# Reciprocal root of a gated recurrence output: quarter-size tile spread by DMA, multiply on GpSimd instead of a combined gate

## What is computed

```python
gg = (x @ Wg.T).reshape(B, L, H, DH)
o = o * jax.lax.rsqrt(jnp.mean(o * o, -1, keepdims=True) + EPS)
o = o * o_norm_w * jax.nn.silu(gg)
return (o.reshape(B, L, KEY_DIM) @ Wo.T, final_state)
```

## Time and profile before

| | us |
|---|---|
| median of 3 runs | 1225.5 (1222.16 to 1226.76) |
| profiled execution | 1221.33 |
| its span | 1219.5 |
| PE busy | 1145.7 (94%) |
| DVE busy | 814.1 (67%) |
| ACT busy | 716.0 (59%) |
| POOL busy | 499.3 (41%) |

### The profile page before, as it was taken

One profiled execution on the slowest core, in us unless ns is written; L12 is line 12 of the kernel. 1 busy time (PEld: TensorE's weight loads), 2 busy tenths in 40 slices (PEclk: granted clock), 3 DMA queues, 4 the chain that ended last, 5 costly groups with the idle time before them and its releaser, 6 DMA issues.

```text
span 1219.5 us, 30002 instructions
## 1 busy us (share of the span) xinstructions
PE 1145.7 (94%) x12192; PEld 790.1 (65%) x12192; DVE 814.1 (67%) x1454; ACT 716.0 (59%) x1212; POOL 499.3 (41%) x709
## 2 busy tenths in 40 slices
PE   7888899999999999999998989859999999999987
PEld 2444455555555555555555556649998998998976
DVE  4897667768768768668576665665665566655552
ACT  3776467677677676776775866624444434445433
POOL 1659576575675774773774811100011000001000
PEclk9999799999999999999998999989999999999999
DMA  3123222323323223243326422161111122111100
GB/s 118 46 52 79 66 52 60 107 58 72 87 58 93 68 73 77 77 128 89 91 73 150 151 62 72 47 235 45 44 45 49 50 52 70 44 44 48 30 17 10
DMA packets 134602, 88.07 MB, mean 72 GB/s; under 512 B 79264, under 2 KB 118048, under 8 KB 133568
## 3 DMA queue, kind: packets, MB, share of 16 engines
q1 hardware_dynamic: 133312, 85.93, 25.9%
q10 hardware_dynamic: 1152, 0.21, 0.1%
HBM read 54.77 MB, written 14.55 MB: 57 GB/s over the span
## 4 chain that ended last, share of the span: by engine, by line
PE 75%; POOL 8%; DVE 5%; issue 4%; ACT 3%; SPq 2%; DMA 2%; ACTq 0%; POOLq 0%; DVEq 0%
PE proj L467 20%; PE out L1494 5%; PE turned_v_chain L1494 5%; PE gram L482 4%; PE turned_v_chain L1560 4%; PE proj L1552 4%; PE proj L1433 4%; POOL inverse L1204 3%; POOL rank_one L1201 3%; PE out L491 2%; PE turned_v_chain L596 2%; PE gram L1468 2%; PE decays L497 2%; PE turned_v_chain L629 2%; DVE conv L992 2%
## 5 line engine op out<-in xcount | busy, mean ns | idle before, releaser
L992 DVE SCALAR_TENSOR_TENSOR conv<-proj,kq_weights,conv 128x504 f32<-128x504 f32 (+2 forms) x261 | 189.9, 731 | 24.4 <-ACT conv L736 17.7
L467 PE MATMUL proj<-xT,vg_weights 128*128 128x512 f32 x384 | 190.6, 620 | 1.8 <-DVE conv L992 1.6
L1791 POOL TENSOR_TENSOR rope<-rope_part,rope_part 128x512 f32<-128x512 f32 x32 | 40.0, 1271 | 364.8 <-DVE rope_part L1730 364.8
L992 DVE SCALAR_TENSOR_TENSOR conv<-proj,vg_weights,conv 128x504 f32<-128x504 f32 (+2 forms) x192 | 140.8, 734 | 44.9 <-ACT conv L736 40.0
L467 PE MATMUL proj<-xT,kq_weights 128*128 128x512 f32 x348 | 164.5, 599 | 0.2 <-DVE conv L992 0.2
L1204 POOL TENSOR_TENSOR inverse<-inverse,rank_one 128x30 f32<-128x30 f32 (+14 forms) x240 | 125.2, 522 | 18.8
L1201 POOL TENSOR_TENSOR rank_one<-inverse 128x30 f32<-128x30 f32 (+14 forms) x240 | 117.7, 490 | 15.9
L467 PEld LDWEIGHTS proj<-xT,vg_weights 128*128 128x128 f32 x384 | 68.4, 192 | 65.6 <-issue 59.8
L467 PEld LDWEIGHTS proj<-xT,kq_weights 128*128 128x128 f32 x348 | 62.4, 190 | 72.8 <-issue 70.3
L1569 ACT ACTIVATE rstd<-rstd 128x1 f32<-128x1 f32 x48 | 9.8, 203 | 142.6 <-DVE rstd L1677 142.6
L482 PEld LDWEIGHTS gram<-keys_q 128*64 128x64 f32 x896 | 57.6, 138 | 54.7 <-ACT keys_q L747 36.4
(11 more groups left out here) (244 smaller groups left out, 2464.0 us busy)
## 6 DMA issues: line engine op xcount, KB each, us to landing
kq_weights<-in_kq_w SPq DMA_DIRECT2D x32, 390.0 KB, 3.5
vg_weights<-in_vg_w SPq DMA_DIRECT2D x32, 390.0 KB, 4.0
o_scratch<-oT SPq DMA_DIRECT2D x32, 256.0 KB, 2.9
o_in<-o_scratch SPq DMA_DIRECT2D x16, 512.0 KB, 4.1
diagonal<-gram_decayed SPq DMA_DIRECT2D x128, 32.0 KB, 1.9
inverse<-inverse SPq DMA_DIRECT2D x32, 128.0 KB, 2.7
q_first<-rope SPq DMA_DIRECT2D x128, 32.0 KB, 1.9
q_second<-rope SPq DMA_DIRECT2D x128, 32.0 KB, 1.9
```

The costliest lines, as they stand in the source:

```text
L467: mm = e.matmul(bank(c, u)[:], w[:, (k * 3 + c % 3) * 128:(k * 3 + c % 3 + 1) * 128], xT[g][:, k, :], start=(k == 0), stop=(k == KD - 1))
L992: e.scalar_tensor_tensor(acc(c, u)[:, :, back:], src[:, :, 0:S - back], weights(c, u)[:, j:j + 1], acc(c, u)[:, :, back:], ALU.mult, ALU.a ...
L1791: e.tensor_tensor(turned[half][:].rearrange("p b r q -> p r b q"), parts[2 * half][:], parts[2 * half + 1][:], op).then_inc(s_turned, 1)
```

## The change

The root no longer goes into the gate. DVE forms `oT` from `OB`, `o_norm_w` and the gate alone, and no longer waits for the root. The sum over partitions is made by four matmuls of 32 output partitions, each for 128 of the 512 columns, so that Ln and Exp run on a 128x128 tile (`rs4`) whose four blocks of 32 partitions hold the four quarters. Four DMAs of SP spread one row of each block over all 128 partitions of `o_rs`. POOL then multiplies `oT` by `o_rs` in all of slots 11 to 42, behind the first part of its elimination cut. The store of `oT` waits for that product, as do the tile phase's waits in PE and ACT (and a new one in DVE). SP's four DMAs stand first in its slot; one kind of preparation store (KRS) moves from the end of a slot to the next slot, behind them.

```diff
@@ sync @@
                 for s in range(SLOTS):
+                    if live(uo):
+                        e.wait_ge(s_rs, uo + 1)
+                        wait(e, s_gr, uo)
+                        for j in range(4):
+                            e.dma_start(o_rs[:, j * TILE:(j + 1) * TILE],
+                                        rs4[RB * j:RB * j + 1, None, :].broadcast_to([1, 128, TILE])).then_inc(d_rs, 16)
+                    rotated = prepare_at(s - 1)
+                    if rotated is not None and rotated[1] == KRS:
+                        prepare_store(*rotated)
                     if live(ua + 1):
...
                     if live(uo):
-                        e.wait_ge(s_og, uo + 1)
+                        e.wait_ge(s_gr, uo + 1)
                         e.dma_start(o_scratch[:, 4 * group(uo):4 * group(uo) + 4, head(uo), :],
...
-                    if now is not None:
+                    if now is not None and now[1] != KRS:
                         prepare_store(*now)
@@ tensor @@
                 def norm(u):
                     e.wait_ge(s_osum, u + 1)
-                    e.matmul(VB, ones_mean[:], o_sum[:], start=True, stop=True).then_inc(s_norm, 1)
+                    for j in range(4):
+                        mm = e.matmul(VB[rows(j), 0:TILE], ones_mean[:, 0:RB], o_sum[:, j * TILE:(j + 1) * TILE],
+                                      start=True, stop=True)
+                    mm.then_inc(s_norm, 1)
@@ scalar @@
                 def silu_gate(u):
-                    wait(e, s_gr, u - 2)
+                    wait(e, s_og, u - 2)
...
                         e.wait_ge(s_norm, uo + 1)
-                        wait(e, s_og, uo)
-                        e.activation(o_rs[:], VB, ACT.Ln, scale=float(2 ** O_SHIFT), bias=guard[:, 0:1]).then_inc(s_ln, 1)
+                        wait(e, d_rs, 64 * uo)
+                        e.activation(rs4[:], VB[:, 0:TILE], ACT.Ln, scale=float(2 ** O_SHIFT), bias=guard[:, 0:1]).then_inc(s_ln, 1)
...
-                        e.activation(o_rs[:], o_rs[:], ACT.Exp, scale=-0.5).then_inc(s_rs, 1)
+                        e.activation(rs4[:], rs4[:], ACT.Exp, scale=-0.5).then_inc(s_rs, 1)
@@ vector @@
-                def scale_gate(u):
-                    e.wait_ge(s_rs, u + 1)
-                    e.wait_ge(s_silu[G], u + 1)
-                    wait(e, s_og, u)
-                    e.tensor_tensor(o_rs[:], flat(gate[u % 3]), o_rs[:], ALU.mult).then_inc(s_gr, 1)
...
                     def gate_output():
-                        if s > U:
-                            scale_gate(uo)
-                        e.wait_ge(s_gr, uo + 1)
+                        e.wait_ge(s_osq, uo + 1)
+                        e.wait_ge(s_silu[G], uo + 1)
...
-                        e.scalar_tensor_tensor(oT[uo % 2][:], OB[:], onorm[:, 0:1], o_rs[:], ALU.mult,
+                        e.scalar_tensor_tensor(oT[uo % 2][:], OB[:], onorm[:, 0:1], flat(gate[uo % 3]), ALU.mult,
                                                ALU.mult).then_inc(s_og, 1)
@@ gpsimd @@
-                    if live(uo) and s <= U:
-                        e.wait_ge(s_rs, uo + 1)
-                        e.wait_ge(s_silu[G], uo + 1)
-                        wait(e, s_og, uo)
-                        e.tensor_tensor(o_rs[:], flat(gate[uo % 3]), o_rs[:], ALU.mult).then_inc(s_gr, 1)
...
                     elif solving:
                         eliminate(h, CUTS[cut][0])
                         if cut == 3:
                             scale_columns()
+                    if live(uo):
+                        e.wait_ge(s_og, uo + 1)
+                        e.wait_ge(d_rs, 64 * (uo + 1))
+                        e.tensor_tensor(oT[uo % 2][:], oT[uo % 2][:], o_rs[:], ALU.mult).then_inc(s_gr, 1)
@@ tile phase: tensor at u4 == 0, scalar at u3 == 0 @@
-                                e.wait_ge(done["o"], U)
+                                e.wait_ge(done["scaled"], U)
@@ tile phase: vector @@
+                        if u3 == 0:
+                            e.wait_ge(done["scaled"], U)
```

7 lines of the change are left out of this document (4 added, 3 removed).

## The result

| us | before | after |
|---|---|---|
| median | 1223.8 (4 runs, 1220.7 to 1226.8) | 1265.9 (4 runs, 1265.3 to 1267.2) |
| ratio after/before, 95% interval | | 1.035 (1.032 to 1.038) |
| profiled execution, its span | 1221.33, 1219.5 | 1267.19, 1265.4 |

Slower, with 1260 forecast and 1230 to 1285 as the range. The medians lie 42 us apart and the two profiled spans 45.9 us, because the profile before is of one of that kernel's fastest executions (its median was 1223.8 to 1226.8 in five groups of runs) and the profile after is of the slowest of four. First the busy line of the page after, for the earlier trace rows; then the table by stretch, for the earlier trace rows and for stretches behind it (columns: stretch, its length, busy time of PE, PEld, DVE, ACT, POOL, PE clock, DMA share, GB/s).

A forecast was written before the change was run, and what follows sets the result against it. PE was taken to bound slots 10 to 31, POOL's chain the stretch up to 705.4 us, and ACT, PE and DVE in turn past 789. -11.0 + 21.8 - 3.5 + 27.2 = +34.5 us: 1255.8 profiled, 1260 as median, range 1230 to 1285.

The forecast's parts named there:

- Slots 37 to 41: Five shorter norm pieces give 2.5 us, PE's shorter waits for DVE about 1: -3.5 us; late weights could give 3 back.
- rival 2: One port for all reads: transfers 2.5 us longer, counted twice in each late stretch, +10 us, 1270; chance 17%.
- Four column tiles: PE in slots 10 to 31: four side by side take 0.44 us, a gain of 0.5 per unit, -11 us for 22.
- Rival 5: Column tiles don't run side by side: +14 us on any outcome, 1274 on the forecast; no chance of its own given.
- It costs nothing, if the four DMAs have landed.: Slots 10 to 31: POOL's multiply fits the idle time before its o_sum addition; the DMAs may take about 13 us.
- The four DMAs, 9.5 us: 9.5 us from first issue to last landing on an empty queue, 7.0 more behind a full one.
- Rival 1: Short DMAs: the four take 4.5 us; still slower, +12 us, median 1237; chance 17%.
- Slots 33 to 36, POOL's chain, +21.8: Late DMAs, the second unit's queued behind large loads, delay POOL's multiplies and elimination: +21.8 us, as the chain is POOL's alone.
- Slots 41 and 42, +27.2: The last unit's DMAs land behind 5 MB of weights, so multiply, attT and nope(2) come late: +27.2 us.
- the sign of ACT idle for 28 us: Sign that the forecast is right: ACT idle some 28 us before L1624.
- Rival 3: Faster: small transfers slip past the large loads and the DMAs are waited for nowhere; median 1214; chance 9%.
- Rival 4: DMAs well over 13 us: norm waits in each of 22 slots, each further us costing 22; chance 4%.

The follow-up runs named there:

- experiment 7: Changed kernel with the four DMAs of slots 11 to 32 issued behind the key and value weights instead of ahead of them; 1267.8 us.
- experiment 9: Changed kernel with eight DMAs of 64 columns in place of four of 128 columns in slots 11 to 32; 1271.8 us.
- experiment 6: Changed kernel with each of the four DMAs reading all 128 partitions of the quarter tile instead of one partition 128 times; 1238.1 us.
- experiment 10: Changed kernel with unit 23 alone (scaled in slot 34) given one 128x512 sum, full-width Ln and Exp and no DMAs; 1259.8 us.
- experiment 12: Against the kernel with unit 23 alone repaired: thirteen large loads moved from the end of slot 33 to behind slot 34's value weights; 1255.4 us.
- experiment 2: Changed kernel with one 128x512 sum, full-width Ln and Exp and no DMAs from slot 33 on, POOL still multiplying; 1213.1 us.
- experiment 4: Changed kernel with SP's large loads moved behind the spread of slot 34 and behind the last spread of slot 42; 1257.6 us.
- experiment 8: Changed kernel with units 30 and 31 alone (slots 41 and 42) given one 128x512 sum, full-width Ln and Exp, no DMAs; 1239.7 us.
- experiment 5: Changed kernel with the four DMAs of slots 33 to 42 issued by ACT in its own queue instead of by SP; 1259.3 us.

## Why the prediction was right, and where its sizes were off

Direction, places and the mechanism of the three large terms were right: a small gain on PE, then two late stretches where a spread lands behind large loads. Slots 37 to 41 were forecast with the wrong sign. Of the 10 us by which the sum misses, some 4 are the choice of the two profiled executions. By number alone, 1265.9 lies nearer to rival 2's 1270 than to 1260. By its terms, on the profiled scale (the two traces also start 1.4 us apart):

| term | predicted | measured |
|---|---|---|
| slots 10 to 31 | -11.0 | -9.2 |
| slots 32 or 33 to 36 | +21.8 | +17.7 |
| slots 37 to 41 | -3.5 | +6.9 |
| slots 41, 42 to the end | +27.2 | +29.1 |
| sum | +34.5 | +44.5 |

- **Four column tiles.** 0.44 us predicted. The next piece starts 0.36 us behind `norm` and itself takes 0.10 longer (622.64 - 620.73 against 608.24 - 606.43), together 0.46. In pairs the eight products of 0.11 us alone would take 0.44, so more than two ran side by side. "TensorEngine Tiling (Array Packing)" of the Trainium skill, section "Theoretical Speedup", allows up to four times for 32 columns, and the trace agrees with that. Rival 5 falls. With a wide source the same slots gain 11.1 us against the kernel before (492.2 to 481.1), the predicted 11; the missing 1.9 us go to the next point.
- **"It costs nothing, if the four DMAs have landed."** Nearly so. The 13 us of cover were counted from an ordinary slot. In one slot of four SP starts the spread 4 to 6 us late, and there no cover is left. That is 1.9 us in all by one profile of each (0.9 to 3.7 by the eight), and the next microsecond of delay costs at once (experiments 7 and 9: 5 to 6 us).
- **The four DMAs, 9.5 us.** 10.3 us in a quiet slot. With 4.4 us for the shortest landing the others follow at (10.3 - 4.4)/3 = 1.97 us, 33 GB/s, where I had 37; in slot 38 the landings come 1.8 to 2.1 us apart. The Trainium skill's page "SBUF — State Buffer", section "Door 1: The DMA port swizzle", has 27.6 GB/s, from which I estimated 11.9 us for four; the trace lies between, and experiment 6 shows the read of one partition to be the cause. Rival 1 falls since the four took 10.3 us and not 4.5; rival 2's size was too large, its mechanism, a slow read side, is the right one.
- **Slots 33 to 36, POOL's chain, +21.8.** The chain was late as predicted (scaling at 659.36, 8 us of lead eaten; the wait of 10 us in slot 34), and it was the bound at slot 37: DVE waited 7.6 us for it. The size was 4 us too large, since the spread landed 11.6 us behind its issue at 672.8, where the prediction has 16.1 (679.7 to 695.8). (A slip without weight: the 8.0 us count from the store, at 657.9, and not from the 658.6 that the text names.) What the step missed is that the chain was not alone. PE's wait for value weights behind the same loads is nearly as late. Without POOL's wait slot 37 starts 10.6 us sooner (experiment 10); without PE's as well it starts no sooner (12), since POOL's chain, held from its start by unit 22's spread, is the bound again.
- **Slots 37 to 41, -3.5.** This step failed, by 10.4 us. It put late weights at 3 us, and those only in the range; they cost about 6. In slot 40 PE waits 3.0 us for value weights and its next group of matmuls takes 3.49 us and not 1.98 (first row below). These weights were issued at 769.11 and landed 8.2 us later; the same ones took 3.3 us in experiment 6, where the spread reads 128 partitions, and nothing waited for them. From the start of slot 37 to the `norm` of slot 42 the kernel of experiment 6 took 80.7 us and experiment 2, without late spreads, 80.9. The changed kernel took 86.9, and experiments 4, 7, 8, 9 and 10, with the same one-partition spreads there, 86.5 to 87.1 (12, at a lower clock, 89.8). The second fence has this stretch in the kernel before, in experiment 6, in experiment 4 and in the changed kernel. Experiments 4 and 6 had the same mean clock, 0.94, and lie 5.8 us apart, so this part is not the clock's. What then remains is the forecast gain of 3.5 us, which experiment 6 doesn't show either (80.7 against 80.0). The clock was 1.00 before and 0.94 there; how much of this part it explains was not separated.

```profile
777.40 3.49 PE L477 MATMUL proj<-xT,vg_weights 128*128 128x512 f32 x4 [3.04 <-DMA vg_weights<-in_vg_w]
```

```profile
709.80:789.80 80.00, 73.41 (x1085) 52.30 (x1084) 49.12 (x86) 53.93 (x88) 10.83 (x9) 1.00 0.23 57
...
708.80:789.50 80.70, 74.59 (x1112) 53.81 (x1112) 46.98 (x81) 50.65 (x88) 16.13 (x13) 0.94 0.28 70
...
719.30:805.80 86.50, 75.94 (x1112) 53.80 (x1114) 47.38 (x82) 50.64 (x88) 16.09 (x13) 0.94 0.45 68
...
719.70:806.60 86.90, 77.75 (x1112) 54.67 (x1115) 46.69 (x81) 50.70 (x88) 16.11 (x13) 0.91 0.43 64
```

- **Slots 41 and 42, +27.2.** `nope(2)` ended 27.4 us later, beyond the 16.8 already lost. That this comes so near to 27.2 is partly luck, since three errors cancel: in the same count the last spread was issued 2.1 us later than forecast (824.73 - 16.8 against 805.9), landed in 16.9 us and not 20.2, and `nope(2)`, at half the clock, took 1.5 us longer. Behind it 1.7 us more were lost, where the clock stood at 0.77 from 860 to 880. ACT's `attT` began 28.2 us later in the same count (842.91 against 797.95), predicted 29.5 (827.4 against 797.95); the sign of ACT idle for 28 us ahead of it came as 20.9. Experiment 8 gives 26 us back, and 31 between the spans.
- **Rival 3** (faster, waited for nowhere): falls; POOL's multiplies waited 179 us in 13 places. **Rival 4**: not reached; the multiply starts 13 to 17 us behind Exp, and a further microsecond costs only in the slots without cover, not in all 22, so its price of 22 us for each microsecond was too high near the edge.

What stays open: the share of the clock in slots 37 to 41, and how large loads hold a spread: with a queue of its own it was hardly faster (13.7 and 15.3 us), and ahead of the loads of slot 34 it was slower (14.4) than behind them (11.6).

## What to carry to other kernels

A broadcast out of one partition runs at the speed of one partition: use it where 10 us of cover are sure and nothing wants that queue, and find the cover in the worst kind of slot, not the common one. A change that pays in the steady part can be switched off where the work runs out; here ten of 32 units kept the old full-width form, and +3.5% became -1.0%. Where a lead is gained, ask what starts at a fixed event all the same: the large loads did. And where two waits are nearly equally late, don't count on the second one's time: taking away the first gave slot 37 10.6 us, the second gave it nothing, because the chain behind the first was the next bound.

## What the runs showed of the hardware

- One DMA of 64 KB read from one partition and written to 128 lands in 6.3 us (median) when four follow one another, and in 2.6 with a source of 128 partitions. While such reads run, the weights issued behind them are late as well: 390 KB of `kq_weights` land in 7.1 us (median) against 3.4 with the wide source and 3.5 in the kernel before. The pages' rows of DMA issues (KB each, median from issue to landing), of the changed kernel and of experiment 6:

```profile
kq_weights<-in_kq_w SPq DMA_DIRECT2D x32, 390.0 KB, 7.1
```

```profile
kq_weights<-in_kq_w SPq DMA_DIRECT2D x32, 390.0 KB, 3.4
```

- Cutting the same bytes into twice as many rows of half the length, in twice as many DMAs, cost 1.1 us for 256 KB.
- Behind the large loads of slots 33 and 41 a spread took 11.6 and 16.9 us with one partition as source and 8.9 and 13.8 with 128 (experiment 6); ahead of them it took 14.4 and 10.6 (experiment 4), and in ACT's queue beside them 13.7 and 15.3 (experiment 5).
- SP needs 2.9 to 5.5 us to issue four of these DMAs in the changed kernel, and for the thirteen loads (sixteen DMAs, since three of them are in two pieces) 12.6 us (660.1 to 672.7) in the changed kernel, 18.6 (664.1 to 682.7) in experiment 4, right behind a spread. ACT needed 6.0 us for four in one slot, in which it did nothing else.
- From 820 to 840 us, with an idle spell of 18 us that began there, TensorE was granted 0.50 of its clock, the lower of its two levels (1.2 GHz of 2.4), and a mean of 0.67 and 0.77 in the 40 us behind. `nope(2)`, right behind the spell, took 3.78 us, where it took 2.24 before.
